# A LoRA router's query on Trainium2: rows added up first and multiplied once, in place of multiplied and then added

## The reference, cut to what matters

```python
base = jnp.einsum('bsi,oi->bso', x, W_org)
q = jnp.einsum('bi,ki->bk', x.mean(axis=1), Wq)
scores = jnp.einsum('bk,ek->be', q, lora_keys) / math.sqrt(K)
coeffs = jax.nn.softmax(scores, axis=-1)
h = jnp.einsum('bsi,eir->bser', x, lora_down)
delta = jnp.einsum('be,bser,ero->bso', coeffs, h, lora_up)
```

## Time and profile before

| | us |
|---|---|
| median of three runs | 1254.35 (1251.49 to 1257.41) |
| the profiled execution, whole | 1259.31 |
| its span from first to last instruction | 1257.5 |
| TensorE busy in the span | 1222.9 (97%) |
| VectorE busy | 821.9 (65%) |
| ScalarE busy | 476.4 (38%) |
| POOL busy | 681.7 (54%) |
| mean granted clock of TensorE | 0.993 |

### The profile page before, as it was taken

The page is one execution under the profiler, slowest core; times in us unless marked ns, Lnnn a source line. Parts: engine busy times, 40 slices in busy tenths (PEclk is TensorE's granted clock), DMA queues, the critical chain, the costliest instruction groups (busy, mean ns, idle before and its releaser), DMA issues.

```text
span 1257.5 us, 16924 instructions
## 1 busy us (share of the span) xinstructions
PE 1222.9 (97%) x6504; PEld 512.1 (41%) x6504; DVE 821.9 (65%) x1417; ACT 476.4 (38%) x826; POOL 681.7 (54%) x300
## 2 busy tenths in 40 slices
PE   8998899999999899999999999999989999999998
PEld 6564444444444322222222222234434444444444
DVE  7997731433456778998999989335538855737622
ACT  4774521000100467777777677743242010010000
POOL 6005898500033478888989889870164553624510
PEclk9999999999999999999999999999989999999999
DMA  9566143311332145453545444443493443523301
GB/s 356 171 245 154 65 134 115 86 34 34 79 129 92 59 96 113 107 117 87 120 106 112 95 103 104 84 84 60 113 213 105 140 126 100 184 85 101 117 15 52
DMA packets 86764, 141.20 MB, mean 112 GB/s; under 512 B 49056, under 2 KB 59296, under 8 KB 82592
## 3 DMA queue, kind: packets, MB, share of 16 engines
q1 hardware_dynamic: 45840, 94.03, 23.7%
q0 software_dynamic: 4608, 33.56, 13.2%
q10 hardware_dynamic: 36240, 12.60, 5.2%
HBM read 85.49 MB, written 10.49 MB: 76 GB/s over the span
## 4 chain that ended last, share of the span: by engine, by line
PE 79%; DVE 12%; DMA 2%; POOL 2%; ACT 2%; issue 1%; ACTq 0%; SPq 0%; POOLq 0%; DVEq 0%
PE bank L641 46%; PE bank L879 9%; DVE mxp L1616 8%; PE bank L866 6%; PE bank L948 5%; PE bank L911 5%; PE bank L666 3%; PE bank L672 3%; DVE xn L1606 2%; DMA stage_c<-w_in 1%; DMA R<-R 1%; POOL R L607 1%; POOL R L629 1%; PE bank L720 1%; POOL X L548 1%
## 5 line engine op out<-in xcount | busy, mean ns | idle before, releaser
L1616 DVE TENSOR_REDUCE mxp<-bank 128x1 f32<-128x512 f32 x512 | 320.6, 680 | 60.6 <-PE bank L866 60.3
L1261 ACT ACTIVATE R<-bank 128x512 f32<-128x512 f32 x512 | 273.9, 602 | 116.7 <-PE bank L948 113.5
L641 PE MATMUL bank<-XTh,R 128*128 128x512 bf16 x896 | 279.3, 381 | 4.7 <-POOL R L629 4.5
L607 POOL TENSOR_TENSOR R<-R 128x2048 f32<-128x2048 f32 x48 | 218.6, 4555 | 35.4 <-ACT R L1261 29.4
L641 PE MATMUL bank<-R 128*128 128x512 bf16 x960 | 209.2, 379 | 0.0
L641 PE MATMUL bank<-XTl,R 128*128 128x512 bf16 x448 | 170.7, 381 | 0.0
L629 POOL TENSOR_TENSOR R<-stage_pair,R 128x1024 bf16<-128x1024 f32 x32 | 75.4, 2371 | 138.6 <-DVE R L1770 84.1
L641 PEld LDWEIGHTS bank<-R 128*128 128x128 bf16 x960 | 93.9, 98 | 113.3
L866 PE MATMUL bank<-R 96*128 96x512 bf16 x352 | 134.6, 382 | 4.6 <-DVE mxp L1616 3.0
L879 PE MATMUL bank<-R,stage_c 128*32 128x512 f32 x1024 | 137.1, 607 | 0.5 <-ACT R L1261 0.5
L948 PE MATMUL bank<-R 98*128 98x512 bf16 x352 | 134.4, 382 | 2.1 <-ACT R L1261 2.1
(11 more groups left out here) (194 smaller groups left out, 1502.0 us busy)
## 6 DMA issues: line engine op xcount, KB each, us to landing
stage_pair<-wts_in SPq DMA_DIRECT2D x35, 512.0 KB, 3.7
R<-R POOLq DMA_DIRECT2D x16, 1024.0 KB, 6.9
stage_pair<-R POOLq DMA_DIRECT2D x16, 1024.0 KB, 7.0
stage_pair<-w_in SPq DMA_DIRECT2D x32, 512.0 KB, 3.5
stage_c<-w_in SPq DMA_DIRECT2D x32, 512.0 KB, 3.6
R<-q_scr SPq DMA_DIRECT2D x48, 128.0 KB, 2.4
XTh<-ctx_t_in SPq DMA_DIRECT2D x11, 512.0 KB, 7.7
XTh<-ctx_nat_in SPq DMA_DIRECT2D x9, 512.0 KB, 3.9
```

Of the source, the lines that this page charges most:

```text
L607: pool.tensor_tensor(PS[(0, 1, 2, 1)[j]], PB[2 * j % 4], PB[2 * j % 4 + 1], ALU.add).then_inc(p_add, 1)
L641: mm = pe.matmul(o, a, m, start=first and a is ah and bs is bh, stop=last and a is al)
L1261: act.activation(PB[kt % 4][:, h * S:(h + 1) * S], bank[t_bank(g, t)][:, :], ACT.Exp, scale=float(HD) ** -0.5).then_inc(exp_done, 1)
L1616: dve.tensor_reduce(mxp[head // REP % 2][:, m, n // 2, n % 2:n % 2 + 1], bank[s_bank(u)][:, :], AX.X, ALU.max).then_inc(s_max, 1)
```

## The change

For every tile, behind its transposes, eight fp32 products of the rows (xn as weights, one column of ones moving) add the tile's rows up, feature by feature, into columns of bank 6; over the four tiles of a batch they accumulate (`row_total`). VectorE copies the batch's 8 columns to x_total (`row_totals`). `lora_query(b)` is then eight fp32 products with the unsplit weights LQW and one moving column, and lora_mean(b) a copy of one column. POOL's split of LQW is gone. The hidden products use banks 0 to 3 in turn; several waits move along with that. scale_rows waits for the row totals (sum_mm) instead of the transposes. On VectorE, row_totals(0) comes between the updates 5 and 6, and lora_mean(0) behind update 7.

```diff
-H_BANK = (7, 0, 6, 7, 1, 6, 7, 2)
-LQ_BANK = (6, 0)
+H_BANK = (0, 1, 2, 3, 0, 1, 2, 3)
+SUM_BANK, LQ_BANK = 6, 7
+LQ_OUT = 320
...
+        x_total = sb("x_total", [P, B * KT], F32)
...
@@ POOL
             add_columns(1)
-            pool.wait_ge(lqw_in, 16)
-            pool.tensor_tensor(lqw_h, LQW[:, :], zero[:, :].to_broadcast([P, KT * P]), ALU.add).then_inc(lqw_hi, 1)
-            pool.wait_ge(lqw_hi, 1)
-            pool.tensor_tensor(lqw_l, LQW[:, :], lqw_h, ALU.subtract).then_inc(lqw_done, 1)
             split_down(2)
@@ TensorE
+            def row_total(t):
+                b = t // TB
+                if t == TB:
+                    pe.wait_ge(total_done, 1)
+                for k in range(KT):
+                    at = b * KT + k
+                    mm = pe.matmul(bank[SUM_BANK][:, at:at + 1], xn[t % 2][:, k * P:(k + 1) * P], onesf[:, 0:1],
+                                   start=t % TB == 0 and k == 0, stop=t % TB == TB - 1, skip_group_check=True)
+                mm.then_inc(sum_mm, 1)
+
             def lora_query(b):
-                pe.wait_ge(t_lo, 2 * TB * (b + 1))
+                pe.wait_ge(lqw_in, 16)
+                pe.wait_ge(total_done, b + 1)
                 for k in range(KT):
-                    r = slice(k * D + b * S, k * D + (b + 1) * S)
-                    w = slice(k * P, (k + 1) * P)
-                    mm = triple([bank[LQ_BANK[b]][:, :]], lqw_h[:, w], lqw_l[:, w], [XTh[:, r]], [XTl[:, r]],
-                                k == 0, k == KT - 1)
+                    mm = pe.matmul(bank[LQ_BANK][:, LQ_OUT + b:LQ_OUT + b + 1], LQW[:, k * P:(k + 1) * P],
+                                   x_total[:, b * KT + k:b * KT + k + 1], start=k == 0, stop=k == KT - 1,
+                                   skip_group_check=True)
                 mm.then_inc(lq_mm, 1)
...
             quantised_tile(3)
+            pe.wait_ge(cb_done, 4)
+            row_total(0)
             turn_behind(1, 1)
+            row_total(1)
             for t in range(4, TT - 1):
                 quantised_tile(t)
                 turn_behind(t - 2, t % 2)
-            pe.wait_ge(cb_done, 4)
-            pe.wait_ge(lqw_done, 1)
+                row_total(t - 2)
             lora_query(0)
             quantised_tile(TT - 1)
             turn_behind(TT - 3, 1)
+            row_total(TT - 3)
             pe.wait_ge(const_in, 48)
             lora_scores(0)
             pe.wait_ge(wt_done, WT_AT["up"])
+            pe.wait_ge(x_up, 2 * (TT - 1))
             lora_hidden(0)
-            pe.wait_ge(x_up, 2 * (TT - 1))
             lora_hidden(1)
             lora_spread(0)
             turn_behind(TT - 2, 0)
-            pe.wait_ge(cv_done, 2)
+            row_total(TT - 2)
+            pe.wait_ge(x_up, 2 * TT)
             lora_hidden(2)
             turn_behind(TT - 1, 1)
+            row_total(TT - 1)
+            lora_hidden(3)
+            pe.wait_ge(cv_done, 2)
+            lora_query(1)
             pe.wait_ge(h_lo, 1)
-            lora_hidden(3)
-            pe.wait_ge(x_up, 2 * TT)
-            pe.wait_ge(h_lo, 2)
-            lora_query(1)
+            pe.wait_ge(t_lo, 2 * TT)
             lora_hidden(4)
             lora_scores(1)
-            pe.wait_ge(h_lo, 3)
+            pe.wait_ge(h_lo, 2)
             lora_hidden(5)
             lora_spread(1)
+            pe.wait_ge(h_lo, 3)
+            lora_hidden(6)
             pe.wait_ge(h_lo, 4)
-            lora_hidden(6)
             lora_hidden(7)
...
-            pe.wait_ge(h_lo, JT + 1)
+            pe.wait_ge(h_lo, JT + 2)
@@ ScalarE, scale_rows(t)
                 if t >= 2:
-                    act.wait_ge(turned, t - 1)
+                    act.wait_ge(sum_mm, t - 1)
@@ VectorE
+            def row_totals(b):
+                dve.wait_ge(sum_mm, TB * (b + 1))
+                dve.tensor_copy(x_total[:, ds(b, KT)], bank[SUM_BANK][:, ds(b, KT)]).then_inc(total_done, 1)
+
             def lora_mean(b):
                 dve.wait_ge(lq_mm, b + 1)
-                dve.tensor_reduce(lq[:, b:b + 1], bank[LQ_BANK[b]][:, :], AX.X, ALU.add).then_inc(co_step, 1)
+                dve.tensor_copy(lq[:, b:b + 1], bank[LQ_BANK][:, LQ_OUT + b:LQ_OUT + b + 1]).then_inc(co_step, 1)
...
-            for t in range(3, TT - 1):
+            for t in range(3, TT - 2):
                 quantised_update(t)
+            row_totals(0)
+            quantised_update(TT - 2)
+            quantised_update(TT - 1)
             lora_mean(0)
-            quantised_update(TT - 1)
             lora_shares(0)
             lo_parts(TT - 2, TT - 2)
             hidden_lo(0)
             hidden_lo(1)
             lo_parts(TT - 1, TT - 1)
+            row_totals(1)
             hidden_lo(2)
             hidden_lo(3)
             lora_mean(1)
...
@@ VectorE, org_norm(t)
                 if t == 0:
-                    dve.wait_ge(turned, TT)
+                    dve.wait_ge(sum_mm, TT)
```

More of the change, by code:

```diff
@@ L194, in build @@
         LQW = stage_c[0]
-        lqw_h, lqw_l = (stage_c[1][:, :].bitcast(BF16)[:, i * KT * P:(i + 1) * KT * P] for i in range(2))
         q_h, q_l = R[0], R[5]
@@ L269, in build @@
         t_lo = sem("t_lo")
-        lqw_hi = sem("lqw_hi")
-        lqw_done = sem("lqw_done")
+        sum_mm = sem("sum_mm")
+        total_done = sem("total_done")
         lq_mm = sem("lq_mm")
@@ L736, in lora_scores @@
                 pe.wait_ge(co_step, 6 * b + 1)
-                pe.matmul(bank[LQ_BANK[b]][0:1, 0:E_LORA], lq[:, b:b + 1], keys[:, :], start=True, stop=True).then_inc(sc_mm, 1)
+                pe.matmul(bank[LQ_BANK][0:1, 64 * b:64 * b + E_LORA], lq[:, b:b + 1], keys[:, :], start=True, stop=True,
+                          skip_group_check=True).then_inc(sc_mm, 1)
             def lora_spread(b):
                 pe.wait_ge(co_step, 6 * b + 6)
-                pe.matmul(bank[LQ_BANK[b]][:, E_LORA:2 * E_LORA], onesf[0:1, :], coef[0:1, 3, ds(b, E_LORA)],
-                          start=True, stop=True).then_inc(bc_mm, 1)
+                pe.matmul(bank[LQ_BANK][:, 64 * b + E_LORA:64 * b + 2 * E_LORA], onesf[0:1, :], coef[0:1, 3, ds(b, E_LORA)],
+                          start=True, stop=True, skip_group_check=True).then_inc(bc_mm, 1)
             def lora_hidden(u):
@@ L1519, in lora_shares @@
                 m, total, inverse = (coefs[0:1, b, i:i + 1] for i in range(3))
-                s8 = bank[LQ_BANK[b]][0:1, 0:E_LORA]
+                s8 = bank[LQ_BANK][0:1, 64 * b:64 * b + E_LORA]
                 dve.wait_ge(sc_mm, b + 1)
@@ L1533, in lora_shares @@
                     rows = slice(i * R_LORA, (i + 1) * R_LORA)
-                    dve.tensor_copy(cvec[rows, ds(b, JT)], bank[LQ_BANK[b]][rows, E_LORA + i:2 * E_LORA:2]).then_inc(cv_done, 1)
+                    dve.tensor_copy(cvec[rows, ds(b, JT)], bank[LQ_BANK][rows, 64 * b + E_LORA + i:64 * b + 2 * E_LORA:2]).then_inc(cv_done, 1)
                 dve.wait_ge(cv_done, 2 * (b + 1))
```

## The result

| | before | changed |
|---|---|---|
| median | 1256.52 us (5 runs) | 1269.65 us (5 runs, 1265.10 to 1272.72) |
| ratio, 95% interval | | 1.0102 (1.0085 to 1.0120) |
| profiled execution, its span | 1259.31, 1257.5 us | 1272.72, 1270.9 us |
| TensorE busy | 1222.9 us | 1235.5 us |

The change makes the kernel slower by 12.8 us (10.7 to 15.1). The forecast was +6.1 us on a base of 1254.35, so 1260.5 us, with a range that ended at 1267.0; a slower kernel had been given a chance of 0.47. All ratios are of fast runs; one execution of `reordered`, 1808 us at a granted clock of 0.65, is not among them.

What follows compares the result with a forecast made beforehand. TensorE, busy 97% of the span, was taken as the bound. Five fp32 groups of 1.74 us less 4.1 gave +4.6, one clock fall made it +6.1, on 1254.35 so 1260.5 us; range 1256.0 to 1267.0.

Steps and rivals of the forecast that it cites:

- The fp32 price: TensorE's cost for eight thin fp32 products, a row_total or new lora_query: two records each at 0.109 us, 1.74 us.
- the upper end of 3.0 us: Dearer fp32 on TensorE: weight loads don't overlap, 3.0 us per group of eight products; +10.9 and one fall, 1266.8 us, chance 0.11.
- rival F: Each fp32 product on TensorE takes four steps of 0.11 us, 3.5 us a group; +15.4, 1269.8 us, chance 0.04.
- A: No slower: fp32 passes on TensorE come at bf16 pace, 0.4 us a group; -0.7 us, 1253.7 us, chance 0.07.
- Totals 0 to 3: row_total groups of tiles 0 to 3 on TensorE, 7.0 us of work: eat idle time; tile 6 ends as before.
- The first wait: TensorE before row_total(4) waits for VectorE's copy row_totals(0), queued behind update(5); idle about 1.2 us.
- The second: TensorE stands 3.4 us in lora_scores(0), as lora_mean(0) moved behind update(7); hidden products start 4.6 us later.
- POOL's saved split: POOL loses two splitting operations, 1.90 us and some 2.1 us; its down and org splits were in time, so no gain.
- the sum of +4.6 us: All LoRA stage terms without the clock: five fp32 groups less 4.1 us, +4.6 us.
- the term of the clock: TensorE's granted clock falls to 0.50 once, before the hidden products, costing 1.5 us; bounds no fall or two (3.1 us).
- both stretches: TensorE stretches nearly without columns, 144.4 to 150.0 and 153.4 to 159.6 us, where the clock might fall; neither exists before.
- rival C: Two falls of TensorE's clock in place of one: +7.7 us, 1262.0 us, chance 0.20.

Runs made afterwards that it cites:

- reordered: Changed kernel with row_totals(0) between the two statistics of update(5), lora_query(0) behind row_total(5), lora_scores(0) behind hidden(0); ratio 1.0036 to the kernel before.
- fill_both: Changed kernel with unused wide bf16 products on TensorE, 16 before lora_scores(0) and 5 before row_total(4)'s wait; ratio 1.0082 to the kernel before.
- vector_sums: Built on reordered: VectorE instead of TensorE adds up tiles 4 to 7, lora_spread(0) stands behind hidden(2); ratio 1.0002 to the kernel before.
- mean_early: Changed kernel with lora_mean(0) moved back ahead of update(7) on VectorE; ratio 1.0073 to the kernel before.
- fill_second: Changed kernel with 16 unused bf16 products of 512 columns filling TensorE's wait before lora_scores(0); ratio 1.0076 to the kernel before.

## Why the prediction was wrong

**What held.** The fp32 price: two records per product, 16 in 1.68 us, forecast 1.74; the upper end of 3.0 us and rival F with four steps (3.5 us) are out, as is A (0.4 us). By the Trainium skill (FP8 and Floating Point Precision, TensorE Precision Notes) a true fp32 product takes four passes through the array. Four steps of 0.11 us are not what the trace shows: the two records of a product cost 0.21 us together, and how many passes lie in a record can't be read from it. Totals 0 to 3 cost next to nothing: 0 to 2 stood in idle time, and tile 6, moved by total 3 to 140.93 us, ran at full clock and ended when it did before. For total 3 the half clock of tile 6 was not the only reason: VectorE's low part, which the next transposes need, was ready only at 143.9 us in both kernels, and they began at 144.4. The first wait, 1.2 us forecast, was 1.05, for the copy behind update(5). The second, 3.4 forecast, was 3.55, for lora_mean(0). No wait stood before total 6, total 7 or lora_query(1). POOL's saved split gave nothing to TensorE. The shift at the last spread was the shift at 350 us. Without the clock the sum of +4.6 us is confirmed row by row.

**What failed** is the term of the clock. "A fall costs 4.98 - 3.45 = 1.5 us ... I take one, at the second." There were two in the profiled execution, 5.1 us together, and two in each of its other traces. I had named both stretches and made rival C of them, but priced each fall by one row in which the half clock lasted 3.2 us. The first fall came while the query was still running, lasted through nearly all of tile 7, and cost 3.6 us. fill_both shows that it didn't need the wait: the clock fell within the thin products when no idle time stood ahead of them. In the forecast they stood as "nearly without columns" and were still given the odds of the gaps of 3.10 us. That the thin totals have a part in it is shown by `reordered` and `vector_sums`: both waits are gone in each, and the clock fell in the first (0.81 from 157 to 163 us) and stayed at 1.00 in the second, which has no totals there. What else those two differ in was not tested apart.

**What was missing** is 3 to 4 us in the rest of the program, which the forecast put at nothing. The means of the three traces of each kernel add up: 9.6 us at the last spread, -0.8 between it and the last attention product (one trace of the changed kernel has no fall there), and 3.9 in the rest make 12.7 us, against 12.8 measured. The range, which ended at 1267.0, allowed for nothing behind the LoRA stage but the spread of a median. Part of the 3.9 us is again the clock, at half for 10.2 us where it was 6.8, and part a wait for a transpose that only the changed kernel has; the cause of both is open. Apart from this, 2.2 us of the distance between 1260.5 and 1269.65 lie in the base: the median of the kernel before was 1254.35 when the forecast was made and 1256.52 in the comparison.

**The rivals.** C named the right mechanism in the LoRA stage (1262.0 forecast). Its shift at the last spread, 7.7 us, was 9.6 in the mean. F's time, 1269.8 us, is the one measured, and that is chance: its price of a group, 3.5 us, was 1.68.

## What to carry to other kernels

A group of products with one moving column looks busy in every row, and yet the clock fell behind such groups as behind idle time: look at the clock there and not only at the busy share. In the part that TensorE bounds, two thin groups next to each other were followed by a fall in every trace read here, with a wait beside them or without. Behind a single group (totals 6 and 7, the queries of vector_sums, the second query) the clock mostly held, but not always: it fell behind total 6 in mean_early and fill_second. When a chain of small steps is rebuilt, look at which long operation each small copy is queued behind on its engine: here two copies of 0.15 us behind layer norm updates of 5.7 us, with the falls beside their waits, cost more than the exchange of the products itself, and moving them gave most of the loss back. The 48 wide bf16 products gave way to 80 thin fp32 ones (160 records). Of these, 32 lay where TensorE had slack, and the other 48 paid for the wide ones evenly: an fp32 product of 128 weight columns cost 0.21 us with one moving column (0.22 with eight), as much as a bf16 product of 512 (3.45 us for 16). Last, when two kernels differ by 1%, count the time at half clock in each stage before a cause is sought there: here it moved the rest by several us between programs that do the same work in it.

## What the runs showed of the hardware

- A stream of fp32 weight loads of 128 columns with one-column products runs at 0.105 us per record (1.68 us for 16) at full clock. With the clock falling inside, 16 of them took up to 2.98 us (fill_both), and 3.20 us at half clock throughout (second trace of the changed kernel, total 1 at 123.28 us).
- The granted clock fell to 0.50 within one-column products with no idle time just ahead of them (fill_both: thin from 144.8 us on, the fall between 147 and 148 us).
- 3.4 us at half clock cost 1.7 us in the mean: between the last spread and the last attention product the traces take 636.1 to 636.8 us without it, 637.8 to 638.3 with it.
- Filling an idle stretch with wide products kept the clock up behind it and let it fall 14 us later, behind the next thin group (fill_second). A fall that is bought off isn't always saved.
- VectorE's sum of a bank of 512 columns into four numbers per partition took 0.67 us, the same as a plain pass over it.
